# Local attention of a 16-sequence hybrid network: the queries' norm moved from a product of the tile into the exponentials' scale

## The reference

```python
q = l2norm(q) * qs
k = l2norm(k) * ksc
q, k = rotary_xpos(q, k)
sim = jnp.einsum('bhwid,bhwjd->bhwij', bq * 8, bk)   # bk, bv: this block and the one before
sim = jnp.where(mask, -jnp.finfo(sim.dtype).max, sim)
attn = jax.nn.softmax(sim, axis=-1)
out = jnp.einsum('bhwij,bhwjd->bhwid', attn, bv)
```

## Time and profile before

| | before |
|---|---|
| median of 3 executions | 1874.98 us (1874.9 to 1876.33) |
| profiled execution, its time | 1867.61 us |
| its span, first to last instruction | 1865.8 us |
| PE busy | 1701.5 us (91% of the span) |
| DVE busy | 1376.7 us (74%) |
| ACT busy | 1315.6 us (71%) |
| POOL busy | 1117.5 us (60%) |
| mean granted TensorE clock | 0.974 of full speed |

### The profile page before, as it was taken

One profiled execution on the slowest core, in us unless ns is written; L12 is line 12 of the kernel. 1 busy time (PEld: TensorE's weight loads), 2 busy tenths in 40 slices (PEclk: granted clock), 3 DMA queues, 4 the chain that ended last, 5 costly groups with the idle time before them and its releaser, 6 DMA issues. The chain is left out here.

```text
span 1865.8 us, 43572 instructions
## 1 busy us (share of the span) xinstructions
PE 1701.5 (91%) x15560; PEld 1101.6 (59%) x15560; DVE 1376.7 (74%) x2369; ACT 1315.6 (71%) x4484; POOL 1117.5 (60%) x1002
## 2 busy tenths in 40 slices
PE   7998899998989999898599999799998899999989
PEld 4664677774657777454244444467776456777645
DVE  4554999983789999355488887699995488999645
ACT  4444788887358888644499998588887537888753
POOL 3554899982479999401222220699996178999620
PEclk7999999999999999999799999999999999999999
DMA  2002111103011110200765652211101202110201
GB/s 63 2 2 60 24 30 25 24 19 82 12 35 31 29 24 19 52 1 16 113 104 92 108 93 30 65 30 34 26 19 47 54 1 53 24 30 19 53 12 45
DMA packets 73214, 74.81 MB, mean 40 GB/s; under 512 B 18772, under 2 KB 56872, under 8 KB 70952
## 3 DMA queue, kind: packets, MB, share of 16 engines
q1 hardware_dynamic: 73000, 72.03, 18.8%
HBM read 27.99 MB, written 10.49 MB: 21 GB/s over the span
## 5 line engine op out<-in xcount | busy, mean ns | idle before, releaser
L498 POOL TENSOR_TENSOR rsum<-pa,pb 128x512 f32<-128x512 f32 x256 | 325.3, 1292 | 54.2 <-DVE pa L416 41.3
L768 ACT ACTIVATE ffn_prob<-sc,ffn_nmax 128x128 f32<-128x128 f32 x928 | 326.7, 387 | 5.3 <-DVE ffn_nmax L700 5.3
L842 POOL TENSOR_TENSOR ffn_prob<-ffn_prob,ffn_rden 128x512 f32<-128x512 f32 x256 | 265.2, 1057 | 75.2 <-DVE ffn_rden L710 75.0
L507 POOL TENSOR_TENSOR rsum<-rsum,ffn_rnt 128x512 f32<-128x512 f32 x256 | 261.4, 1042 | 10.9 <-ACT ffn_rnt L790 8.6
L768 ACT ACTIVATION_READ_ACCUMULATOR ffn_prob<-sc,ffn_nmax 128x1 f32 x928 | 210.5, 227 | 0.0
L426 DVE TENSOR_TENSOR pb<-proj,ffn_tab 128x512 f32<-128x512 f32 x236 | 161.1, 683 | 59.0 <-ACT rn L468 58.2
L406 PE MATMUL pt<-ident,rsum 128*128 128x128 f32 x960 | 154.6, 284 | 15.2 <-POOL rsum L507 12.5
L700 DVE TENSOR_REDUCE ffn_nmax<-sc 128x4 f32<-128x512 f32 x232 | 148.4, 680 | 13.6 <-PE sc L611 10.4
L406 PEld LDWEIGHTS pt<-ident,rsum 128*128 128x128 f32 x960 | 101.0, 141 | 96.7 <-ACT ffn_ptb L776 70.5
L621 PE MATMUL pt<-ident,ffn_prob 128*128 128x128 f32 x1024 | 144.5, 278 | 14.4 <-POOL ffn_prob L842 14.1
L1718 ACT ACTIVATE column_E<-proj,column_nm 128x256 f32<-128x256 f32 x256 | 123.4, 510 | 44.1 <-DVE column_nm L1642 43.7
(11 more groups left out here) (272 smaller groups left out, 4368.2 us busy)
## 6 DMA issues: line engine op xcount, KB each, us to landing
ffn_v<-ffn_v SPq DMA_DIRECT2D x128, 128.0 KB, 2.3
column_ks<-qk_parts SPq DMA_DIRECT2D x64, 128.0 KB
rn<-Y SPq DMA_DIRECT2D x32, 128.0 KB, 2.3
qk_parts<-column_hi SPq DMA_DIRECT2D x64, 64.0 KB, 2.0
qk_parts<-column_lo SPq DMA_DIRECT2D x64, 64.0 KB, 2.0
column_qs<-qk_parts SPq DMA_DIRECT2D x32, 128.0 KB
column_qs<-qk_parts SPq DMA_DIRECT2D x64, 64.0 KB
rn<-Y SPq DMA_DIRECT2D x32, 127.5 KB, 2.4
```

The lines of the kernel that those rows point to most:

```text
L498: pool.tensor_tensor(K.sm[:, r, w], K.m1[:, r, w], K.m2[:, r, w], ALU.add).then_inc(S.f_sum, 1)
L507: pool.tensor_tensor(heads(K.sm[:, r, w]), heads(K.sm[:, r, w]), K.rnt[:, r, w * HEADS:(w + 1) * HEADS].unsqueeze(2).broadcast_to([P, HEAD ...
L768: ins = act.activation(K.prob[:, r, e, k], score_banks(i)[e][:, tokens(k)], ACT.Exp, bias=K.nmax[:, r, e, k:k + 1], accum_out=K.den[:, r, ...
L842: pool.tensor_tensor(K.prob[:, r, e], K.prob[:, r, e], K.rden[:, r, e].unsqueeze(2).broadcast_to([P, 4, P]), ALU.mult).then_inc(S.f_pn, 1)
```

## The change

The queries are no longer multiplied by their inverse norms. `scale` on POOL treats the keys alone. The transposes of a query tile wait for its sum (`f_sum`) in place of its product (`f_scl`). The raw maxima of both heads go to a new tile `nraw`; a third DVE instruction multiplies the 128x8 raw maxima by the rows' inverse norms and writes `nmax`. The eight exponentials of a chunk take the inverse norm as a per-row scale, and all of them wait for the product. `rnt` grows from two tiles to two pairs of four, since a norm is now read up to a pair later. The mask's constant changes from -1e30 to -1e25.

```diff
 def transposes(pe, K, n, j, w, bank):
-    pe.wait_ge(S.f_scl, 2 * TILES * n + 2 * j + (2, 1)[w])
+    if w == 0:
+        pe.wait_ge(S.f_sum, 2 * TILES * n + 2 * j + 1)
+    else:
+        pe.wait_ge(S.f_scl, TILES * n + j + 1)
...
 def scale(pool, K, n, j):
-    for w in (1, 0):
-        pool.wait_ge(S.f_sum, 2 * TILES * n + 2 * j + w + 1)
-        pool.wait_ge(S.f_rn, TILES * n + j + 1)
-        pool.tensor_tensor(heads(K.sm[:, r, w]), heads(K.sm[:, r, w]),
-                           K.rnt[:, r, w * HEADS:(w + 1) * HEADS].unsqueeze(2).broadcast_to([P, HEADS, DH]),
-                           ALU.mult).then_inc(S.f_scl, 1)
+    q, t = divmod(j, 4)
+    pool.wait_ge(S.f_sum, 2 * TILES * n + 2 * j + 2)
+    pool.wait_ge(S.f_rn, TILES * n + j + 1)
+    pool.tensor_tensor(heads(K.sm[:, r, 1]), heads(K.sm[:, r, 1]),
+                       K.rnt[:, q % 2, t, HEADS:2 * HEADS].unsqueeze(2).broadcast_to([P, HEADS, DH]),
+                       ALU.mult).then_inc(S.f_scl, 1)
...
             def maxima(i):
                 for e in range(2):
                     dve.wait_ge(S.f_sc, 2 * TILES * n + 2 * i + e + 1)
-                    dve.tensor_reduce(K.nmax[:, i % 2, e], blocks(score_banks(i)[e][:]), AX.X, ALU.max, negate=True).then_inc(S.f_mx, 1)
+                    if e == 0 and i >= 1:
+                        dve.wait_ge(S.f_mx, TILES * n + i)
+                    dve.tensor_reduce(K.nraw[:, e], blocks(score_banks(i)[e][:]), AX.X, ALU.max, negate=True).then_inc(S.f_raw, 1)
+                p, c = divmod(i, 4)
+                dve.wait_ge(S.f_raw, 2 * TILES * n + 2 * i + 2)
+                dve.tensor_tensor(K.nmax[:, i % 2], K.nraw[:], K.rnt[:, p % 2, :, 2 * c:2 * c + 2].rearrange("p k e -> p e k"),
+                                  ALU.mult).then_inc(S.f_mx, 1)
...
             def exponentials(i):
+                p, c = divmod(i, 4)
+                act.wait_ge(S.f_mx, TILES * n + i + 1)
                 for e in range(2):
-                    act.wait_ge(S.f_mx, 2 * TILES * n + 2 * i + e + 1)
...
                         ins = act.activation(K.prob[:, r, e, k], score_banks(i)[e][:, tokens(k)], ACT.Exp,
-                                             bias=K.nmax[:, r, e, k:k + 1], accum_out=K.den[:, r, e, k:k + 1])
+                                             bias=K.nmax[:, r, e, k:k + 1],
+                                             scale=K.rnt[:, p % 2, k, 2 * c + e:2 * c + e + 1], accum_out=K.den[:, r, e, k:k + 1])
...
             def inverse_norms(j):
-                if j >= 2:
-                    act.wait_ge(S.f_scl, 2 * TILES * n + 2 * (j - 1))
-                act.activation(K.rnt[:, j % 2], K.lss[:], ACT.Exp, scale=-0.5, bias=K.rsb[:]).then_inc(S.f_rn, 1)
+                q, t = divmod(j, 4)
+                if q >= 2:
+                    act.wait_ge(S.f_scl, TILES * n + j - 7)
+                    act.wait_ge(S.f_ex, 2 * TILES * n + 8 * (q - 1))
+                act.activation(K.rnt[:, q % 2, t], K.lss[:], ACT.Exp, scale=-0.5, bias=K.rsb[:]).then_inc(S.f_rn, 1)
```

More of the change, by code:

```diff
@@ L33 @@
 EPS_LN = 1e-5
-MASKED = -1e30
+MASKED = -1e25
 SS_SCALE = 2.0 ** 40
@@ L914, in _ @@
                     pool.wait_ge(S.f_cl, TILES * (n + 1) + j + 1)
-                    pool.tensor_tensor(K.rnt[:, j % 2], K.ssc[:], K.mhalf[:].broadcast_to([P, 2 * HEADS]), ALU.pow).then_inc(S.f_rn, 1)
+                    pool.tensor_tensor(K.rnt[:, j // 4, j % 4], K.ssc[:], K.mhalf[:].broadcast_to([P, 2 * HEADS]), ALU.pow).then_inc(S.f_rn, 1)
                     if j < LEAD - 1:
@@ L1771, in __init__ @@
         self.f_sc = new("f_sc")
+        self.f_raw = new("f_raw")
         self.f_mx = new("f_mx")
@@ L1883, in ffn @@
         K.lss = sb("lss", [P, 2 * HEADS])
-        K.rnt = sb("rnt", [P, 2, 2 * HEADS])
+        K.rnt = sb("rnt", [P, 2, 4, 2 * HEADS])
+        K.nraw = sb("nraw", [P, 2, 4])
         K.nmax = sb("nmax", [P, 2, 2, 4])
```

## The result

The changed kernel takes 1950.53 us as a median of four runs (1948.04 to 1953.87), the kernel before 1874.94 beside it (four runs, 1867.35 to 1876.33). The ratio is 1.0414, with a 95% interval of 1.0395 to 1.0432: the change costs 4.1%, 76 us by the medians. The profiled execution of the changed kernel took 1953.87 us with a span of 1952.1, 86.3 above the span of before. Of all executions in this document one, of `scale_fixed`, fell into a slower state (2053.93 us at a mean granted clock of 0.795), and the ratios leave it out.

The account below looks back on a forecast made before the run. PE's pace of 7.34 us a step, stretched by POOL, bounds the kernel; the ACT and DVE loop takes over at 7.86. 11.8 + 4.8 + 0.8 + 3.4 = 20.8 a block, x 4 = 83, less 3: +80, median 1955 us, range 1888 to 1985.

Parts of the forecast that it names:

- PE's own pace of 7.34: Attention steps of the kernel before: PE alone needs 7.34 us a step, stretched by POOL in steps with `low_parts`.
- 3.5 us a block to win from POOL: Six steps a block with `low_parts`: a lighter POOL gives back PE's 0.58 us stall in each.
- The slack loop of 6.92: One-step loop through ACT and DVE: 6.92 us, 0.42 under PE's pace; the change makes it 7.86, setting the pace.
- The second operand, 0.092 each: ACT's eight exponentials a step: the per-row scale adds 0.092 us each, 0.74 a step.
- The product, 0.20: DVE after the maxima: the new 128x8 product adds 0.20 us a step, bounds 0.12 and 0.35.
- The product blocked in `low_parts` steps, 0.8: DVE's product waits 0.8 us for POOL in six steps a block: +4.8 us a block, bounds 0 and 7.7.
- 27 steps: Pipelined part of each attention block: 27 x 7.86 = 212.2 us against 200.4, +11.8 a block, before contention.
- The tail: Block end: chunks 27, 28, 31 pay for the scale, chunk 30 waits longer, ACT falls behind; +3.4 us a block.
- Starts and openings, +0.8 a block and -3: First exponentials wait for second maximum and product, +0.8 us a block; POOL's sums start sooner opening blocks 0 and 2, -3 together.
- Never meets POOL: Rival: the scale costs its full price, but DVE's product slips past POOL; +61 us, 1936; chance 0.15.
- faster: Rival: POOL's stall goes and ACT and DVE's loop stays under PE, scale at most 27 ns; -11 us, 1864; chance 0.08.
- Operand free, contention not: Rival: the scale costs nothing and PE's pace stays, but POOL blocks DVE's product; +17 us, 1892; chance 0.12.

Follow-up runs that it names:

- scale_fixed: The changed kernel with the constant 1.0 as the exponentials' scale in place of the per-row operand, product kept; 1860.4 us, ratio 0.9951 to the kernel before.
- before_low_split: The kernel before with `low_parts` cut into two halves, run on POOL in two neighbouring steps; 1859.49 us, ratio 0.9947.
- low_after_product: The changed kernel with `low_parts` held on POOL until the same step's product of the maxima is done; 1932.91 us, ratio 1.0338.
- order: The changed kernel with ACT's Ln and Exp of a tile moved behind the next tile's squares; 1898.97 us, ratio 1.0161 to the kernel before.
- before_ones_scale: The kernel before with every exponential given a per-row scale from a column of ones; 1905.16 us, ratio 1.0191.

## Why the prediction was right, and where it was off

Forecast were 1955 us, 1888 to 1985, and slower with 0.89; measured 1950.5. From profile to profile the forecast was +80 and the measurement 86.3, from median to median 76. The mechanism was right; that the sum came so near is in part luck, since the 77.0 us of the four blocks hold some 5 of lower clock (three tails at 1.5, and 1.0 in the third block's steps, an estimate) that the forecast did not have.

- **PE's own pace of 7.34 and 3.5 us a block to win from POOL.** The pace was right: `scale_fixed` runs its 27 steps at 7.33 and gains 0.5%, and `before_low_split` gains as much without the change. The 3.5 was too much. The steps that follow a stall were shorter for it, and 27 x 7.34 is 198.2, only 2.2 under the 200.4 of before; the two kernels won 2.4 and 2.7 a block.
- **The slack loop of 6.92.** Right: it is the loop that now binds, and it measured 7.86 in an ordinary step, as forecast, and 7.94 in the steps in which PE's scores end after the sine product (0.06 of the difference).
- **The second operand, 0.092 each.** Right. From one exponential to the next it is 0.43 or 0.44 in place of 0.35, the interval to the read grew by 0.10, and the first to `keep_output` takes 3.50, as said. The profile's duration of an exponential grew by less, from a mean of 387 ns to 463. The Trainium skill ("ScalarE: Activation LUTs", section "What ACT_TABLE_LOAD costs") has some 93 ns for each per-partition pointer operand; by the distance between exponentials, 0.08 to 0.10 us more, the trace now agrees for a second one too. `scale_fixed` shows that this term decides the sign.
- **The product, 0.20.** Right, 0.24 with its handovers, where 0.23 was put down.
- **The product blocked in `low_parts` steps, 0.8.** The mechanism was right, the size was off: 0.65, since a blocked product doesn't wait 0.80 (321.07 - 320.27) and then take its 0.17; it ends 0.02 after POOL's instruction, so that most of its own time lies inside the wait. 6 x 0.65 = 3.9 a block where 4.8 was forecast. `low_after_product` gives back 14.2 us (4.14 - 3.38 = 0.76%, by 18.7) where four blocks by 3.9 are 15.6. In its profile the 27 steps take 211.6, 4.3 less a block, since the first step alone falls by 1.05. The Trainium skill ("SBUF — State Buffer", sections "Who interferes with whom" and "Summary: rules for kernel authors") says that of a DVE instruction with two SBUF inputs and a GpSimd one that reads SBUF the later one is blocked fully. The trace agrees for a product of 128x8 and one of 128x4, whose ends come 0.02 behind POOL's.
- **27 steps.** Forecast 212.2 + 4.8 = 217.0 us, measured 215.9 (216.9 in the third block, where two steps take 8.82 and 8.26 and the granted clock of the first of them is 0.97). **The tail** grew by 3.7, 2.9, 3.9 and 3.3, forecast 3.4; where the clock was alike, as in the windows shown, it is 2.9. Together 77.0 in the four blocks, forecast 80.
- **Starts and openings, +0.8 a block and -3.** The start was right: from the opening's last sums to the first normalise it is 10.14 us in place of 9.36. The openings' term was twice too large: their steps did become shorter (sums at 189.20, 194.33, 199.54, 204.76, 209.97: 5.13 to 5.22, before 5.38), but by 0.8 over the four steps of the first block where 1.5 was forecast. The 9.3 us ahead of the blocks' first normalise, forecast +0.2 together, are another matter: 3.7 of them were there before a changed instruction ran, and the granted clock is lower in one of the other stretches (0.97 in place of 0.98 ahead of the fourth block). What the rest is, no run settled.
- **The rivals.** *Never meets POOL* fell with the row of 0.82. The *faster* one was right about its condition: with the operand free, 1860 was measured where 1864 was forecast, and the ratios agree (0.9951 and 0.994). *Operand free, contention not*, 1892, wasn't a real case: at PE's pace the product gets in 0.03 us ahead of `low_parts`. I had taken the queue's length as fixed and the product's place in it as independent of the pace. The same wrong step gave the miss on `scale_fixed`.

The costs don't add up: operand, order, product and gate, each taken away alone, give back 4.6, 2.5, 1.7 and 0.8 points, 9.6 of 4.1. Each works on the same loop, and as soon as it is under PE's pace the rest is worth nothing. For the same reason the operand costs 87 us in the changed kernel (4.63% of 1870) but 35 in the kernel before.

## What to carry to other kernels

Before work is moved off a busy engine, add up every loop of dependences that the new place lies in, and compare its slack with the price: here 0.42 us of slack met 0.94 us of new work, to spare an engine whose stall was worth 0.1 us a step on average (2.4 to 2.7 in 27). A per-row operand on many short activations is not free, even where it takes the place of a whole product elsewhere. If a rare long item makes an engine stall, split it over neighbouring steps first, and keep small two-input operations of DVE clear of POOL's long ones by order or a gate.

## What the runs showed of the hardware that I had not expected

- A 0.17 us DVE product took 0.82 behind a POOL instruction that had begun before it (up to 1.27 over the whole kernel), and starting it 0.7 us sooner only moved it behind another POOL instruction (0.63). Whether it is hit at all hung on 0.03 us in one version.
- A scale of ones from a column costs as much as one that differs by row: a mean of 471 ns in `before_ones_scale`, 463 in the changed kernel, 385 with a constant. It is the operand that is paid for, not its values.
- On POOL, 128x512 products took 1.04 us with one operand broadcast from 128x8, and 1.27 with two full inputs; a 128x256 half of the latter took 0.72 or 0.73, so about 0.17 of the 1.27 comes again with each instruction, which is an estimate from these rows.
